# Attention scores made once, with the powers turned by a transposing DMA

## The reference

```python
xf = x.reshape(B, Cc, H * W)
f = jnp.einsum('kc,bcn->bkn', Wq, xf) + bq[None, :, None]
g = jnp.einsum('kc,bcn->bkn', Wk, xf) + bk[None, :, None]
h = jnp.einsum('oc,bcn->bon', Wv, xf) + bv[None, :, None]
s = jnp.einsum('bki,bkj->bij', f, g)
beta = jax.nn.softmax(s, axis=1)
o = jnp.einsum('bci,bij->bcj', h, beta)
o = gamma[0] * o
```

## Time and profile before

| | |
|---|---|
| time, median of 3 runs (lowest, highest) | 2233.79 us (2233.73, 2235.2) |
| the profiled execution: span from first to last instruction | 2231.2 us |
| busy: TensorE, VectorE, ScalarE, GpSimd | 2185.2, 1851.9, 1663.5, 632.1 us |
| granted TensorE clock, mean | 0.998 |

### The profile page before, as it was taken

The page is one execution under the profiler, slowest core; times in us unless marked ns, Lnnn a source line. Parts: engine busy times, 40 slices in busy tenths (PEclk is TensorE's granted clock), DMA queues, the critical chain, the costliest instruction groups (busy, mean ns, idle before and its releaser), DMA issues.

```text
span 2231.2 us, 42620 instructions
## 1 busy us (share of the span) xinstructions
PE 2185.2 (98%) x16782; PEld 1621.5 (73%) x16782; DVE 1851.9 (83%) x3100; ACT 1663.5 (75%) x2686; POOL 632.1 (28%) x614
## 2 busy tenths in 40 slices
PE   4899999999999999999999999999999999999999
PEld 3577777777777777777777777777787777777754
DVE  7788888888888888888888888888887778788677
ACT  5577777777777777777777777777877777777877
POOL 2100111112232342333522233443333222132246
PEclk9999999999999999999999999999999999999999
DMA  5000000000012222211222122221201111110112
GB/s 197 13 1 1 1 9 8 9 17 1 20 50 66 78 72 62 62 46 47 56 74 75 43 55 67 76 73 52 57 15 50 40 35 38 31 38 15 49 38 76
DMA packets 60231, 101.06 MB, mean 45 GB/s; under 512 B 8800, under 2 KB 15712, under 8 KB 60000
## 3 DMA queue, kind: packets, MB, share of 16 engines
q1 hardware_dynamic: 60032, 98.34, 15.5%
HBM read 71.83 MB, written 19.92 MB: 41 GB/s over the span
## 4 chain that ended last, share of the span: by engine, by line
PE 95%; DVE 3%; ACT 1%; DMA 1%; SPq 0%; issue 0%; POOL 0%; DVEq 0%
PE acc L1604 19%; PE acc L1596 19%; PE acc L1597 19%; PE tps L1403 10%; PE sps L1419 10%; PE tps L1470 3%; PE acc L1397 3%; PE tps L1472 2%; PE acc L1470 1%; PE tps L1434 1%; PE tps L1456 1%; PE tps L1384 1%; PE acc L1472 1%; DVE mx L726 1%; PE acc L1581 1%; PE acc L1583 1%
## 5 line engine op out<-in xcount | busy, mean ns | idle before, releaser
L1181 ACT ACTIVATE ph<-sps,esc 128x512 f16<-128x512 f32 x1024 | 703.8, 687 | 406.6 <-PE sps L1419 401.4
L1596 PE MATMUL acc<-hth,ph 128*128 128x257 f16 x3968 | 926.4, 274 | 0.1
L1597 PE MATMUL acc<-htl,ph 128*128 128x256 f16 x3968 | 925.5, 273 | 0.0
L726 DVE TENSOR_REDUCE mx<-tps 128x1 f32<-128x512 f32 x1024 | 700.5, 686 | 270.6 <-PE tps L1403 263.0
L745 DVE TENSOR_TENSOR pl<-p,ph 128x512 f16<-128x512 f32 x1024 | 797.9, 780 | 33.0 <-ACT p L1182 31.7
L1182 ACT ACTIVATE p<-sps,esc 128x512 f32<-128x512 f32 x1024 | 699.8, 683 | 0.0
L1604 PE MATMUL acc<-hth,pl 128*128 128x257 f16 x3968 | 600.5, 273 | 0.0
L1604 PEld LDWEIGHTS acc<-hth,pl 128*128 128x128 f16 x3968 | 387.3, 98 | 153.5 <-issue 0.3
L1597 PEld LDWEIGHTS acc<-htl,ph 128*128 128x128 f16 x3968 | 388.5, 98 | 145.3 <-issue 0.3
L996 POOL TENSOR_TENSOR xl<-xn,xh 128x512 f16<-128x512 f32 x176 | 227.5, 1313 | 855.9 <-DVE xn L707 831.7
L1596 PEld LDWEIGHTS acc<-hth,ph 128*128 128x128 f16 x3968 | 388.6, 98 | 60.8 <-ACT ot L1187 2.4
(11 more groups left out here) (240 smaller groups left out, 1680.0 us busy)
## 6 DMA issues: line engine op xcount, KB each, us to landing
rt<-turned SPq DMA_DIRECT2D x96, 256.0 KB, 4.7
xt<-x SPq DMA_DIRECT2D x36, 512.0 KB, 3.7
xb<-x SPq DMA_DIRECT2D x32, 512.0 KB, 4.8
out<-zt SPq DMA_DIRECT2D x45, 256.0 KB, 2.1
yb<-turned SPq DMA_DIRECT2D x36, 128.0 KB, 2.7
rt<-turned SPq DMA_DIRECT2D x72, 64.0 KB, 4.8
turned<-yb SPq DMA_DIRECT2D x12, 256.0 KB, 2.0
out<-fst SPq DMA_DIRECT2D x8, 256.0 KB, 2.0
```

The costliest lines, as they stand in the source:

```text
L726: V.reduce_max(mx[:, tile, c:c + 1], tps[par][:], AX).then_inc(t_free[par], 1)
L1181: A(ph[:, u % SLOTS], sps[u % 2][:], ACT.Exp, scale=esc[:]).then_inc(ph_ok, 1)
L1596: mm(acc[j][:, 0:C + 1], w, hth[:, t], start=(t == 0), stop=False)
L1597: mm(acc[j][:, 0:C], w, htl[:, t], start=False, stop=False)
```

## The change

The change rewrites the attention steps:

- The scores are made once, with places j on partitions. A unit is 128 places j by 1024 places i: two score matmuls of 512 columns into a pair of PSUM banks (`ring`, three pairs). There are 4 units to 128 places j, 128 in a batch, 512 in all. A span is two units; w counts spans, and two spans (one tile g) finish 128 places j.
- VectorE takes the maximum of a unit (`most`), joins two of them and makes a bias (`shift`), and ScalarE exponentiates with that bias, with 1024 columns to an instruction: `high_part` to float16, `full_part` to float32, with the sum of the powers collected by the same instruction. The two spans of a tile have different biases; `ratio`, `first_half` and `join` put them together, and `sums` and `divide` end a block.
- The powers now have places i as columns, but must be weights with places i on partitions. Two transposing DMAs to a unit (`turn`, one for the high halves, one for the low ones, 128 by 1024 float16 each) write them turned into pt (three slots). SyncE issues them in its one list.
- In a unit TensorE takes eight blocks of 128 places i, each with three matmuls of 256 columns (`attend_quarter`).
- The low half of a unit is made by VectorE, except for every fourth unit, where GpSimd makes it.
- Pieces, maxima ahead of a block, the row of shifts and its matmuls, and the column of ones are gone. xn, in which a normed input waits for its low half, has one slot for two. Jobs around the steps are moved to other step numbers, and `project` no longer holds pieces. SyncE's jobs are written out span by span.

```diff
+UNIT = 2 * CH
+UNITS = HW // UNIT
+RINGS = 3
+STORES = 3
+TURNED = 3
+WHOLE = 2
 GRING = 10
 RING = 4
-STEPS = NCH * NT
+BLOCKS = UNIT // P
...
+        ring = ctx.enter_context(nc.psum_tensor("ring", [P, RINGS, UNIT], f32))
         tps = [ctx.enter_context(nc.psum_tensor(f"tps{i}", [P, CH], f32)) for i in range(2)]
+        bank = [ring[:, i // 2, i % 2 * CH:(i % 2 + 1) * CH] for i in range(2 * RINGS)]
+        acc, sps = bank[0:4], bank[4:6]
...
+        def by_pool(u):
+            return u % 4 == 3
+        def low_made(u):
...
+            def turn(u):
+                sp.wait_ge(ph_ok, u + 1)
+                if u >= TURNED:
+                    sp.wait_ge(p_free, u - TURNED + 1)
+                sp.dma_start_transpose(pt[:, u % TURNED, 0:BLOCKS],
+                                       pb[:, u % STORES, 0]).then_inc(th_in[u % TURNED], 16)
+                sp.wait_ge(*low_made(u))
+                sp.dma_start_transpose(pt[:, u % TURNED, BLOCKS:2 * BLOCKS],
+                                       pb[:, u % STORES, 1]).then_inc(tl_in[u % TURNED], 16)
...
-            def piece_max(tile, c, par):
-                full(par)
-                V.reduce_max(mx[:, tile, c:c + 1], tps[par][:], AX).then_inc(t_free[par], 1)
-            def step_piece(u):
-                if u + AHEAD < ALL:
-                    piece_max((u + AHEAD) // NCH % NT, u % NCH, 0)
-            def tile_max(G):
-                if G:
-                    dve.wait_ge(m_rows, G)
-                for par in range(2):
-                    dve.wait_ge(t_free[par], filled[par])
-                carry_wait()
-                t = G % NCH * QT
-                V.tensor_reduce(nm[:], mx[:, t:t + QT], AX, ALU.max, negate=True).then_inc(nm_ok, 1)
...
+            def most(u):
+                dve.wait_ge(s_mm, u + 1)
+                V.tensor_reduce(mx[:, u % 4:u % 4 + 1], ring[:, u % RINGS], AX, ALU.max).then_inc(mx_ok, 1)
+            def shift(n):
+                dve.wait_ge(mx_ok, 2 * n + 2)
+                at = 2 * n % 4
+                V.scalar_tensor_tensor(top[:], mx[:, at:at + 1], mx[:, at + 1:at + 2], nesc[:], ALU.max,
+                                       ALU.mult).then_inc(top_ok, 1)
+                dve.wait_ge(top_ok, n + 1)
+                if n % 2:
+                    V.tensor_scalar(nb[:, n % 8:n % 8 + 1], top[:], EXP_SHIFT, nb[:, n % 8 - 1:n % 8], ALU.add,
+                                    ALU.min).then_inc(nb_ok, 1)
+                else:
+                    V.tensor_scalar(nb[:, n % 8:n % 8 + 1], top[:], EXP_SHIFT, None, ALU.add).then_inc(nb_ok, 1)
             def low_part(u):
                 dve.wait_ge(p32_ok, u + 1)
-                V.tensor_tensor(pl[:, u % SLOTS], p32[:, u % SLOTS], ph[:, u % SLOTS],
-                                ALU.subtract).then_inc(pl_ok, 1)
-            def divide(G, some):
-                for j in some:
-                    if j + 1 < QT:
-                        dve.wait_ge(acc_mm, G * (QT - 1) + j + 1)
-                    else:
-                        dve.wait_ge(p_free, (G + 1) * NT)
-                    V.reciprocal(rinv[:, j:j + 1], acc[j][:, C:C + 1]).then_inc(rinv_ok, 1)
-                    if j >= 2:
-                        dve.wait_ge(rinv_ok, G * QT + j + 1)
-                        V.tensor_scalar(ot[:, j], acc[j][:, 0:C], rinv[:, j:j + 1], None,
-                                        ALU.mult).then_inc(ot_dve, 1)
+                if u >= STORES:
+                    dve.wait_ge(tl_in[(u - STORES) % TURNED], times_turned(u - STORES))
+                V.tensor_tensor(pb[:, u % STORES, 1], p32[:, u % WHOLE], pb[:, u % STORES, 0],
+                                ALU.subtract).then_inc(pl_dve, 1)
...
+            def join(g):
+                dve.wait_ge(p_free, UNITS * (g + 1))
+                dve.wait_ge(tq_ok, g + 1)
+                V.tensor_tensor(ot[:, g % (QT + 1)], tps[1][:, 0:C], tq[:], ALU.add).then_inc(ou_ok, 1)
...
-            def split_max(n):
-                pool.wait_ge(nm_ok, n + 1)
-                if n:
-                    pool.wait_ge(m_mm, n)
-                step(tt(r3[:], nm[:], mw[:, 4], ALU.add))
-                step(tt(mrow[:, :, 96], r3[:], mw[:, 2], ALU.mult))
-                step(tt(r2[:], mrow[:, :, 96], mw[:, 0], ALU.mult))
-                step(tt(r1[:], r3[:], r2[:], ALU.subtract))
-                tt(mrow[:, :, 97], r1[:], mw[:, 3], ALU.mult).then_inc(m_rows, 1)
...
+            def low_part(u):
+                pool.wait_ge(p32_ok, u + 1)
+                if u >= STORES:
+                    pool.wait_ge(tl_in[(u - STORES) % TURNED], times_turned(u - STORES))
+                tt(pb[:, u % STORES, 1], p32[:, u % WHOLE], pb[:, u % STORES, 0], ALU.subtract).then_inc(pl_pool, 1)
...
-            def powers(u):
-                act.wait_ge(s_mm, u + 1)
-                if u >= SLOTS:
-                    act.wait_ge(p_free, u - SLOTS + 1)
-                A(ph[:, u % SLOTS], sps[u % 2][:], ACT.Exp, scale=esc[:]).then_inc(ph_ok, 1)
-                A(p32[:, u % SLOTS], sps[u % 2][:], ACT.Exp, scale=esc[:]).then_inc(p32_ok, 1)
+            def high_part(u):
+                act.wait_ge(nb_ok, u // 2 + 1)
+                if u >= STORES:
+                    act.wait_ge(th_in[(u - STORES) % TURNED], times_turned(u - STORES))
+                    act.wait_ge(*low_made(u - STORES))
+                k = u // 2 % 8
+                A(pb[:, u % STORES, 0], ring[:, u % RINGS], ACT.Exp, bias=nb[:, k:k + 1],
+                  scale=esc[:]).then_inc(ph_ok, 1)
+            def full_part(u):
+                k, g = u // 2 % 8, u // UNITS
+                col = (0, 2, 1, 3)[u % UNITS]
+                if u >= WHOLE:
+                    act.wait_ge(*low_made(u - WHOLE))
+                A(p32[:, u % WHOLE], ring[:, u % RINGS], ACT.Exp, bias=nb[:, k:k + 1], scale=esc[:],
+                  accum_out=lu[:, g // QT % 2, col, g % QT:g % QT + 1]).then_inc(p32_ok, 1)
+            def ratio(g):
+                act.wait_ge(nb_ok, 2 * g + 2)
+                k = 2 * g % 8
+                A(al[:, g // QT % 2, g % QT:g % QT + 1], nb[:, k:k + 1], ACT.Exp, bias=nb[:, k + 1:k + 2],
+                  scale=-1.0).then_inc(al_ok, 1)
...
+            def first_half(g):
+                act.wait_ge(p_free, UNITS * g + 2)
+                act.wait_ge(al_ok, g + 1)
+                act.wait_ge(ou_ok, g)
+                A(tq[:], tps[0][:, 0:C], ACT.Copy, scale=al[:, g // QT % 2, g % QT:g % QT + 1]).then_inc(tq_ok, 1)
...
-            def piece(b, tile, c, par):
-                free(par)
-                fill(mm(tps[par][:], gst[0:96, key_tile(b * NT + tile)], fst[0:96, b % 2, c * CH:(c + 1) * CH],
-                        start=True, stop=True), par)
-            def step_piece(u):
-                if u + AHEAD < ALL:
-                    g, c = divmod(u + AHEAD, NCH)
-                    b, tile = divmod(g, NT)
-                    if b and tile == 0:
-                        pe.wait_ge(fg_in[0], spreads(b, c))
-                    piece(b, tile, c, 0)
             def scores(u):
-                if u >= 2:
-                    pe.wait_ge(p32_ok, u - 1)
-                G, tile = divmod(u, NT)
-                mm(sps[u % 2][:], fst[:, G // NCH % 2, tile * P:(tile + 1) * P], gst[:, keys_at(G)], start=True,
-                   stop=True).then_inc(s_mm, 1)
-            def rows(G, bank):
-                pe.wait_ge(m_rows, G + 1)
-                for q in range(QT):
-                    last = mm(bank[:, q * P:(q + 1) * P], mrow[:, q], idh[:], start=True, stop=True)
-                last.then_inc(m_mm, 1)
+                w = u // 2
+                b, c = w // PER_B, u % UNITS * 2
+                if u >= RINGS:
+                    pe.wait_ge(p32_ok, u - RINGS + 1)
+                if w % PER_B < 2:
+                    for par in range(1 if b else 2):
+                        pe.wait_ge(fg_in[par], spreads(b, c + par))
+                for e in range(2):
+                    last = mm(ring[:, u % RINGS, e * CH:(e + 1) * CH], gst[0:96, key_tile(w // 2)],
+                              fst[0:96, b % 2, (c + e) * CH:(c + e + 1) * CH], start=True, stop=True)
+                last.then_inc(s_mm, 1)
+            def attend_quarter(w, q):
+                u = 2 * w + q // 2
+                g, s = divmod(w, 2)
+                if q == 0 and g:
+                    pe.wait_ge(ou_ok if s else tq_ok, g)
+                o, i = tps[s][:, 0:C], u % UNITS * BLOCKS
+                if q % 2 == 0:
+                    pe.wait_ge(th_in[u % TURNED], times_turned(u))
+                for k in range(6 * (q % 2), (6, 8)[q % 2]):
+                    mm(o, pt[:, u % TURNED, k], hth[:, i + k], start=(q == 0 and k == 0), stop=False)
+                    mm(o, pt[:, u % TURNED, k], htl[:, i + k], start=False, stop=False)
+                if q % 2:
+                    pe.wait_ge(tl_in[u % TURNED], times_turned(u))
+                    for k in range(BLOCKS):
```

(16 more changed lines are left out.)

686 lines of the change are left out of this document (294 added, 392 removed), and 9 rows, old and new, of the table ORDER.

## The result

The changed kernel took 2313.81 us (median of 4 runs, 2304.87 to 2328.06), the kernel before 2234.49 beside it: ratio 1.036 [1.033, 1.040], 80 us slower. The forecast was 2045 us, and faster; the sign was wrong too. The stated range, 1980 to 2400 us, holds the result only because it had been stretched into the slow case.

What follows compares the result with a forecast made beforehand. The prediction took TensorE to bound the kernel: 2231.2 us of span, less 225 and 12, is 1994; 48 for SyncE's bursts makes 2042, and 2.6 around it 2045 us. The range was 1980 to 2400 us.

Steps and rivals of the forecast that it cites:

- Cost on the path: 0: GpSimd's low halves, 2.6 us each, 128 times, cost nothing, because each is wanted two spans after its power.
- I take 0.93: DMA engines: a 256 KB transposing transfer priced at 0.93 us, because bytes and rows are like those of plain copies.
- all is hidden: DMA queue: a unit's two transposes need 1.9 us of 3.06, so they add no time.
- some 3 us of slack: What two issues of up to 0.93 us and a landing of 2.1 to 3 us leave before turned blocks are wanted.
- The bound c = 1.85 of the rival on the other side: SyncE's list and DMA queue: transposes above 1.85 us each make the kernel slower, by 340 + 1024 c; chance 0.26.
- c of 2.0 us: The time per transpose that the range's upper end, 2400 us, stands for.
- charge of 48 us for bursts: SyncE's list: 1 us for each of 24 query and key groups and 24 rotated-copy groups that pass the slack.
- TensorE's work: Attention matmuls: from 1024 steps of 1.75 us to 512 units of 3.06 us, 225 us less, plus 12 for the shift row.
- The sum on the accumulator: ScalarE's full power: collecting the sum in the same instruction, in no row, was taken as costing nothing.
- The coupled loop: VectorE and ScalarE handing over in turns: 5.9 us a span against TensorE's 6.1, so priced at 0.
- a rival at 2200: The loop over VectorE and ScalarE sets the pace, 6.7 us or more a span, about 2200 us; chance 0.20.
- 1994 + 2.6: Whole kernel: 1994 us of span if nothing else stops TensorE, and 2.6 us around it.

Runs made afterwards that it cites:

- e4: The changed kernel with all low halves on VectorE, none on GpSimd: 2244.18 us.
- e6: The changed kernel with all low halves on VectorE and only high halves turned, used twice by TensorE: 2111.32 us.
- e1: The changed kernel without the transposing transfers of the low halves; TensorE takes the turned high halves twice: 2213.07 us.
- e16: The changed kernel with GpSimd's five layer 1 products moved behind the next block's first low half: 2302.29 us.
- e8: Transfers measured alone, no layer computed: 1.59 us per transposing 128x1024 with two in flight, 1.11 us per plain copy of 256 KB.
- e5: e4 with the join placed ahead of the span's first low half in VectorE's order: 2241.81 us.
- e7: e4 with layer 1's rotated copies issued by ScalarE's queue instead of SyncE's: 2305.51 us.
- e9: e5 with layer 1's rotated copies issued between transposing transfers instead of in a row: 2212.65 us.
- e12: e5 with one transposing transfer of 128x2048 for both halves of a unit instead of two: 2360.92 us.
- e13: e9 with the next unit's high half transferred before this unit's low half in SyncE's order: 2309.42 us.
- e10: e4 without loading layer 1's rotated copies; the products use other operands: 2159.35 us.
- e3: The changed kernel without loading layer 1's rotated copies; GpSimd multiplies the projected channels by themselves: 2219.58 us.
- e11: e6 without the sum accumulated by the full power, row sums being a constant: 2106.79 us.
- e17: e6 plus a GpSimd subtraction of 128x1024 for every fourth unit, on constants, that nobody reads: 2293.95 us.

## Why the prediction was wrong

**GpSimd, "Cost on the path: 0".** This step failed. The prediction asked whether GpSimd would be late, and the rows that it used already had the other question in them: a low half of 512 columns took VectorE 681 ns alone and 810 in the mean with GpSimd busy. It took those 129 ns as spread over all of them. The source row of the same stretch of the kernel before (minimum, median and maximum) says otherwise; most aren't touched, and a few last about twice as long:

```profile
L745 DVE TENSOR_TENSOR pl<-p,ph x31: 677/681/1333, 800.3 to 860.8; 128x512 f16<-128x512 f32 x31
```

What the runs show is a hold to the end of GpSimd's instruction, and that had become 2.17 us long instead of 1.3. The collision hits `top`, on which ScalarE's two powers and then everything wait. Measured 70 us (e4 against the changed kernel) to 102 (e6 against e1); lateness is some 12 of the 70 (e16). The Trainium skill says it in a line ("GPSIMD Engine Reference", Key points): GpSimd shares its SBUF interfaces with VectorE, and contends with VectorE instructions that have two SBUF inputs. The trace agrees, in `top` (held) and the maximum from PSUM (not held, 1.22 us beside GpSimd). The prediction should have weighed it.

**The transposes, "I take 0.93" and "all is hidden".** The price was off, and with it the overlap: 1.35 us of the engines alone (e8) and, in the changed kernel, (0.842 x 2303 - 0.155 x 2231) / 1024 = 1.56 us, taking the other traffic as in the earlier trace rows; and an issue of 1.27 to 1.33 us, where up to 0.93 was allowed, with a landing of 3.3 to 3.4 us where 2.1 to 3 was. The "some 3 us of slack" is then 6.1 - 1.3 - 3.3 = 1.5 us for a high half (an estimate), before SyncE waits for anything. They were priced as copies because the bytes are alike; the plain copy is 0.62 x 1.11 = 0.69 us of the engines, half as much. The 350 to 400 GB/s of the Trainium skill ("Advanced Engine Details and Errata", X-Bar Transpose), quoted in the prediction, isn't reached here: 163 GB/s at a share of 0.85, some 190 if it were 1.

**The bound c = 1.85 of the rival on the other side** failed as well. With c = 1.59 that rival's own formula gives 340 + 1024 x 1.59 = 1968 us, not slower, and yet the kernel is. The slow end of the range was "c of 2.0 us", which wasn't measured, so that 2314 lies inside the range is luck. The formula treated the queue as a rate, averaged over the kernel: fast enough or not. But a unit's block goes from power to low half to transfer to TensorE and back through three buffers, and with a queue wanted for 88% of the time or more, what stands ahead of it becomes a wait. Five kernels with nearly the same work and traffic, e5, e7, e9, e12 and e13, lie from 2213 to 2361 us by the order, grouping and issuer of the transfers. The charge of 48 us for bursts was the right idea and too small: the copies' groups, charged 24 us, are worth 85 to 94 (e10, e3), 29 of which come back by spreading them out (e9), and leaving out the low halves' transfers, with SyncE's waits for low halves, gives 101 to 133 (e1, e6). As a rate, too, the queue should have been taken by stage. In batch 1 of e9 the engines are busy for 0.95 x 533 = 506 us, where the forecast left TensorE 511 - 128 x 0.44 - 3 = 452. How much of the loss in batches 1 to 3 is this rate and how much the order isn't separated: e6, with a share of 0.62, still takes 509 us for the same batch.

**What held.** TensorE's work: 24 x 0.11 + 2 x 0.21 was right to about 1%, as its busy time shows where little disturbs it (1970.6 us in e6, 2185.2 - 225 - 12 = 1948 forecast). ScalarE, VectorE and GpSimd per large operation: 1.20 us against 1.11 for a power, 1.22 against 1.22 for a maximum, 2.17 against 2.6 for GpSimd's low half. The sum on the accumulator, priced 0, is worth 5 us (e11).

**The coupled loop, priced at 0 and a rival at 2200.** With half of the transfers and no GpSimd, e6 is still 115 us over 1994 + 2.6. Some 22 of these are TensorE's busy time, and the rest idle time (139 us against 46 before). The longest waits of TensorE in it are those for the ring and the join, 28 us each, and VectorE is busy for 88% of a stretch of batch 1 (441 of 500 us). That this loop through VectorE is the cause is argued, not shown. For it speaks e17, which lengthens VectorE's work by 181 us and the time by 183; but no run shortened VectorE's part, and e11, which takes 105 us out of ScalarE's, gives only 5.

**In sum**, from below (the split depends on the order, as the two causes aren't additive): 1997 forecast without bursts, + 114 (hand-overs and busy time, e6) = 2111, + 133 (the low halves' transfers and SyncE's waits for low halves, e4) = 2244, + 70 (GpSimd's share) = 2314. The clock is in these terms, not beside them: TensorE's busy time for the same 15630 instructions is 1970.6 us in e6 at a mean granted clock of 0.992 and 2026.9 in the changed kernel at 0.968, 56 us more, as more of it falls to the lower of the clock's two levels, 1.2 and 2.4 GHz: busy time times clock is 1955 us in the one and 1962 in the other. The prediction had named that as a sign and put no price on it.

## What to carry to other kernels

Work given to a second engine isn't free because that engine has room: look at what else uses its way to memory, and at the shortest instruction on the loop that would stand behind it. With a queue that is wanted 88% of the time, latency and order count beside the rate; take its rate by stage, price what stands ahead of a block by its longest burst and by what the list itself waits for, and measure an operation that no row shows by itself before counting on it. When each large operation costs what was forecast and the sum doesn't hold, look through the small ones for a mean far from its median.

## What was new about the hardware

- A VectorE instruction with two operands in SBUF, of one column, lasted up to 3.36 us beside GpSimd's instructions and ended with them (201.36 against 201.34 us; 206.30 against 206.28 with unrelated data; 105 of the 108 stretched ones within 0.06 us), where 0.22 is usual. The longest was held through three of GpSimd's instructions in a row, to 610.44, 612.52 and 613.19 us, and ended at 613.20. The maximum from PSUM didn't stretch (1204 to 1225 ns in 512).
- A transposing transfer of 128x1024 f16 within SBUF: 1.35 us of the 16 engines, 3.0 to 3.3 us from issue to landing, 1.23 to 1.33 us of SyncE's queue in the median; a plain one of the same bytes 0.69, 2.3 and 0.47. Half of the columns halves the engines' time (0.50 x 1.31 = 0.66 us), not the issue (1.27).
- At equal bytes the packet time of all DMAs (share times span) was 1939 to 1948 us in the changed kernel, e4, e5 and e9, whose spans run from 2206 to 2303 us; with the copies on ScalarE's queue (e7) it was 2046. A share of 0.97 in a stretch didn't mean that a better order had nothing to give (e5 to e9, 29 us).
